# Two small remainders in one tile of a routed expert layer, with the second expert's weights fetched

## The chip, the cores and the metric

The kernel runs on one core of a Trainium2 chip. The metric is the device time of one execution in microseconds; the time before is the median of three runs.

## What is computed

The input `x` (4 x 256 tokens, 256 channels) first gets a gated mixing term, and then a gated expert layer. The second one is what matters here. There are T = 1024 tokens, H = 256 channels, E = 32 experts with M = 176 inner channels, and each token goes to 6 experts:

```python
scores = jax.nn.sigmoid(xf @ w_router)
# 4 of 8 groups of experts by scores + corr_bias, then 6 experts among these
combine = zeros((T, E)).at[arange(T)[:, None], topk_idx].add(topk_w)
g = einsum('th,ehm->etm', xf, gate_w)
u = einsum('th,ehm->etm', xf, up_w)
eo = einsum('etm,emh->eth', silu(g) * u, down_w)
routed = einsum('te,eth->th', combine, eo)
shared = silu(xf @ sh_gate_w) * (xf @ sh_up_w) @ sh_down_w
x = x + tanh(g_ffn[0]) * (routed + shared)
```

Everything is in float32. How many tokens an expert gets is known only when the kernel runs.

## The kernel before

The first part (about a third of the time) computes the mixing term, the router, the choice of experts and the shared expert. The expert with the most tokens in the first half is treated apart: all 1024 tokens go through it (`gate_up_busy`, `turn_h_busy`, `down_busy`). All other pairs of token and expert are written as rows to a buffer in HBM, `rows_dram`, each expert's rows in a region of its own (L429 `place`, indirect DMAs of GpSimd). On VectorE a table is worked out (L1074 to L1116): tile t of 128 rows belongs to expert `tiles[0, t]` and begins at row `tiles[1, t]`. An expert's remainder under 128 rows takes a tile of its own. The tiles are cut into rounds of `ROUND = 8`, and `last`, the number of the last round, comes from the table at run time: `last_i` is the number of entries of `round_at` (16, 24, ...) that lie under the number of tiles, and `load_last` (L255) adds 1.

The main loop goes tile by tile. All weights lie in SBUF (`wgu`, `wd`), and the engines work one behind the other:

- SyncE (SP queue), and ScalarE's queue up to tile 31, loads the 128 rows of tile t into one of 8 buffers (L259 `load`), once tile t - 8 has been transposed (`s_xT`) and taken (`s_taken`). From round `HELD = 4` on this is the loop at L354, all on SP.
- TensorE, at step t (L806 `iteration`), does four things in this order: `transpose_x` of tile t + 2 (L736), `gate_up` of tile t + 1 (L742, two matmuls of 352 columns, `pG`), `turn_h` of tile t (L750) and `down` of tile t - 1 (L756, two matmuls of 256 columns, `pY`). Rounds 0 and 1 are written out, then comes a loop over all rounds that are possible with an `If` in it (L837), then the last round.
- ScalarE copies the transposed rows (L547), applies silu (L552) and scales the result with the token's weight (L559 `scale_y`).
- VectorE, at step t (L1174 `turn`), copies the transposed h of tile t (L1134), gates tile t + 1 (L1130), and takes from tile t + 1's rows the weights and the token numbers (L1136 `take`, the lines L1140 and L1143, which count `s_taken` up).
- GpSimd adds each tile's result to the rows of one of three sums in HBM, by token number (L436 `add`, L445, an indirect DMA with addition). Two adds into one sum may not overlap, so each waits until the one before it into its sum has landed.

After the last round SP reads the three sums back (L367), VectorE adds them (L1197, L1203), and the output is written (L371).

Another piece that the steps use: at L313 `weights_of_busy` fetches one expert's weights by a number read at run time, in four DMAs on SP.

The reference's own inputs, counted apart from the kernel, give this: without the expert treated apart there are 32 full tiles, 8 remainders of more than 64 tokens and 16 remainders of 1 to 64 tokens, so 56 tiles in 7 rounds.

## Time and profile before

| | us |
|---|---|
| median of three runs | 258.53 (258.03 to 259.87) |
| profiled execution, its own time | 258.77 |
| its span | 256.9 |
| TensorE busy | 219.3 (85%) |
| GpSimd busy | 157.4 (61%) |
| VectorE busy | 129.4 (50%) |
| ScalarE busy | 80.0 (31%) |

The span is what the profiler saw between the first and the last instruction; the execution's own time is 1.9 us longer. Busy times are sums over an engine's instructions. PE is TensorE, PEld its weight loads, DVE VectorE, ACT ScalarE, POOL GpSimd, SP SyncE. Matmuls are recorded with modelled ends that overlap; in the chain of work the overlap is taken out. A float32 matmul stands as two records.

### The profile page before, as it was taken

How to read it: one execution, taken by the hardware profiler on the slowest of the kernel's cores; microseconds unless marked ns; L12 is line 12 of the kernel's file. 1: busy time of each engine (PE TensorE's matmuls, PEld its weight loads, DVE VectorE, ACT ScalarE, POOL GpSimd, SP SyncE). 2: the span in 40 equal slices, each digit the busy share in tenths (PEclk: the TensorE clock that was granted, in tenths of full speed). 3: DMA queues.
4: the chain of work that ended last, by engine and by line, in shares of the span. 5: the costliest groups of instructions: out<-in, count | busy, mean ns of one | idle time of the engine just before them, and what ended most of it. 6: DMA issues, size and time to landing. Idle time of an engine off the chain costs nothing.

```text
span 256.9 us, 5093 instructions
## 1 busy us (share of the span) xinstructions
PE 219.3 (85%) x1043; PEld 170.9 (67%) x1044; DVE 129.4 (50%) x528; ACT 80.0 (31%) x222; POOL 157.4 (61%) x188
## 2 busy tenths in 40 slices
PE   7996987994799789999999999999999998996000
PEld 6895776882677467877777777778777776774000
DVE  2898886929554444434443444434343443343334
ACT  3636121011010124343434344344444433442000
POOL 6352888787878873528468488566575665475300
PEclk9779799997599999999999999999999999999555
DMA  6999999999997649999998768777667675257767
GB/s 200 250 260 278 407 376 331 332 373 292 318 351 255 195 151 337 253 303 214 249 231 158 126 112 154 121 121 119 107 117 108 110 119 81 35 64 153 175 168 260
DMA packets 41018, 53.72 MB, mean 209 GB/s; under 512 B 5134, under 2 KB 35438, under 8 KB 40998
## 3 DMA queue, kind: packets, MB, share of 16 engines
q1 hardware_dynamic: 25520, 30.99, 41.7%
q0 software_dynamic: 11280, 18.36, 35.7%
q10 hardware_dynamic: 4198, 4.15, 5.9%
q8 instruction: 7, 0.11, 0.3%
q14 instruction: 13, 0.11, 0.1%
HBM read 31.72 MB, written 21.77 MB: 208 GB/s over the span
## 4 chain that ended last, share of the span: by engine, by line
PE 61%; DVE 17%; DMA 8%; issue 5%; another core or an unknown queue 4%; POOL 4%; ACT 1%; SPq 0%; ACTq 0%; POOLq 0%; DVEq 0%
PE pG L742 26%; PE pY L756 18%; PE pX L736 5%; DMA sum_dram<-xnT,idx 5%; PE pH L750 5%; PE pG L765 3%; PE pY L692 2%; PE pY L784 2%; DMA wgu<-sum_dram 2%; POOL rows_dram L432 1%; DMA wij<-in_L_xattn_W_dram 1%; PE pH L773 1%; DVE wgu L1013 1%; POOL rstd L418 1%
## 5 line engine op out<-in xcount | busy, mean ns | idle before, releaser
L445 POOL DMA_INDIRECT sum_dram<-xnT,idx x56 | 86.7, 1548 | 57.2 <-ACT xnT L559 30.8
L742 PE MATMUL pG<-wgu,sdown 128*128 x224 | 75.8, 461 | 1.4 <-issue 1.4
L432 POOL DMA_INDIRECT rows_dram<-rows,row_i x48 | 47.5, 989 | 18.3 <-issue 11.3
L756 PE MATMUL pY<-wd,sup 88*128 x224 | 57.5, 379 | 0.0
L1134 DVE COPY sup<-pH 88x256 f32<-88x256 f32 x56 | 23.5, 420 | 59.0 <-PE pH L750 51.3
L742 PEld LDWEIGHTS pG<-wgu,sdown 128*128 128x128 f32 x224 | 38.5, 191 | 13.9 <-issue 2.0
L559 ACT ACTIVATE xnT<-pY,wt 128x256 f32<-128x256 f32 x56 | 26.5, 473 | 54.1 <-issue 22.4
L756 PEld LDWEIGHTS pY<-wd,sup 88*128 88x128 f32 x224 | 38.0, 190 | 3.2 <-issue 0.2
L750 PEld LDWEIGHTS pH<-ident,sgate 128*88 128x88 f32 x112 | 18.0, 161 | 13.6 <-DVE sgate L1130 0.5
L552 ACT ACTIVATE sgate<-pG 128x176 f32<-128x176 f32 x56 | 17.8, 317 | 27.1 <-PE pG L742 26.0
L547 ACT ACTIVATE sdown<-pX 128x256 f32<-128x256 f32 x56 | 21.0, 377 | 4.9 <-PE pX L736 4.5
L750 PE MATMUL pH<-ident,sgate 128*88 128x128 f32 x112 | 21.5, 273 | 0.0
L1130 DVE TENSOR_TENSOR sgate<-sgate,pG 128x176 f32<-128x176 f32 x56 | 18.1, 323 | 0.1
L692 PE MATMUL pY<-sdown,wgu 128*128 128x256 f32 (+1 forms) x48 | 13.9, 448 | 4.9 <-DVE wgu L1013 3.4
L681 PE MATMUL pG<-xnT,sgate 128*128 128x256 f32 (+1 forms) x48 | 13.8, 413 | 3.6 <-DVE wgu L1013 3.6
L692 PEld LDWEIGHTS pY<-sdown,wgu 128*128 128x128 f32 (+1 forms) x48 | 10.6, 225 | 7.9 <-DVE wgu L1013 4.2
L519 ACT ACTIVATE wgu<-pG 128x256 f32<-128x256 f32 (+1 forms) x12 | 4.6, 383 | 29.8 <-PE pG L681 18.4
L681 PE MATMUL pG<-xnT,sup 128*128 128x256 f32 (+1 forms) x48 | 13.8, 415 | 0.0
L681 PEld LDWEIGHTS pG<-xnT,sgate 128*128 128x128 f32 (+1 forms) x48 | 8.5, 192 | 5.7 <-DVE wgu L1013 4.5
L736 PEld LDWEIGHTS pX<-ident,rows 128*128 128x128 f32 x56 | 10.6, 196 | 2.0 <-issue 0.7
L736 PEld LDWEIGHTS pX<-ident,xg 128*128 128x128 f32 x56 | 10.9, 195 | 1.3
L736 PE MATMUL pX<-ident,rows 128*128 128x128 f32 x56 | 10.9, 278 | 0.3 <-issue 0.3
(183 smaller groups left out, 246.2 us busy)
## 6 DMA issues: line engine op xcount, KB each, us to landing
wgu<-in_L_ffn_gate_w_dram SPq DMA_DIRECT2D x8, 704.0 KB, 10.0
wgu<-in_L_ffn_up_w_dram SPq DMA_DIRECT2D x8, 704.0 KB, 13.0
wd<-in_L_ffn_down_w_dram SPq DMA_DIRECT2D x8, 640.0 KB
sum_dram<-zeros POOLq DMA_DIRECT2D x3, 1152.0 KB
wgu<-sum_dram SPq DMA_DIRECT2D x12, 256.0 KB, 3.9
xg<-rows_dram SPq DMA_DIRECT2D x16, 144.5 KB
rows<-rows_dram ACTq DMA_DIRECT2D x16, 144.5 KB
rows_dram<-zeros SPq DMA_DIRECT2D x8, 289.0 KB, 4.5
```

The lines of the kernel that those rows point to most:

```text
L432: pool.indirect_dma_start(rows_dram[:, :], bass.IndirectOffsetOnAxis(ap=row_i[:, j, k:k + 1], axis=0), lines[:, j * ROW:j * ROW + LINE], N ...
L445: pool.indirect_dma_start(sums_dram[into[s]][:, :], bass.IndirectOffsetOnAxis(ap=idx[:, s:s + 1], axis=0), y[s], None, compute_op=ALU.add) ...
L547: nc.scalar.activation(xT[:, par, :, :].rearrange("p k t -> p (k t)"), pX[par][:, 0:K * P], ACT.Copy).then_inc(s_xTc, 1)
L559: nc.scalar.activation(y[s], pY[s % 2][:, 0:H], ACT.Copy, scale=wt[:, s:s + 1]).then_inc(s_yc, 1)
L681: ins = nc.tensor.matmul(pG[u % 2][0:m, i * GROUP * P:(i + 1) * GROUP * P], w[:, k, c], xnT[:, k, b * GROUP * P:(b + 1) * GROUP * P], star ...
L692: ins = nc.tensor.matmul(pY[j % 2][:, 0:H], sh[0:m, b % 2, i, (j % GROUP) * P:(j % GROUP + 1) * P], sdown[0:m, i, :], start=(i == 0), stop ...
L736: ins = nc.tensor.transpose(pX[par][:, k * P:(k + 1) * P], xg[s][:, 0:H].rearrange("t (p k) -> t k p", k=K)[:, k, :], ident[:, :])
L742: ins = nc.tensor.matmul(pG[par][:, 0:2 * M].rearrange("t (g m) -> t g m", g=2), xT[:, par, k, :], wgu[:, bass.ds(e, 1), :, k, :].rearrang ...
L750: ins = nc.tensor.transpose(pH[par][0:MI, i * P:(i + 1) * P], h[:, par, :].rearrange("t (p i) -> t i p", i=I)[:, i, :], ident[:, :])
L756: ins = nc.tensor.matmul(pY[par][:, 0:H], hT[0:MI, par, i, :], wd[:, bass.ds(e, 1), i, :], start=(i == 0), stop=(i == I - 1))
L1130: V.tensor_tensor(h[:, par, :], sg[:, par, :], pG[par][:, M:2 * M], ALU.mult).then_inc(s_h, 1)
L1134: V.tensor_copy(hT[0:MI, par, :, :].rearrange("p i t -> p (i t)"), pH[par][0:MI, 0:I * P]).then_inc(s_hTc, 1)
```

## The change

Remainders of up to `SIDE = 64` tokens no longer take a tile of 128 rows each. The last round but one (`last - 1`) is a round of 8 shared tiles: the upper 64 rows belong to one expert, the lower 64 rows to another one, whose table entries are at `SHARED + s` and `SHARED + 8 + s`. Full tiles and remainders over 64 tokens take the other rounds (small ones beyond 16 too). The number of rounds is then that of the whole tiles, divided by 8 and rounded up, and one more: with the counts above 40 / 8 + 1 = 6.

In a shared tile, `gate_up_sides` and `down_sides` do each matmul of a whole tile as two matmuls of 64 columns of the weight side, one for each expert, the second into output partitions 64 to 127 with `tile_position=(0, 64)`. The first expert's weights are read from where all lie; those of the second are fetched again from HBM into fixed places of SBUF: three places for gate and up (`own_gu`, 2 DMAs of 176 KB each time), two for down (`own_d`, 2 DMAs of 160 and 16 KB). These places overlay tables of the routing that are no longer needed (`choice` in place of eleven tensors). The first three pairs of gate and up and the first two of down are issued before round 4; the rest stand in SP's program between the row loads of the final round (`load_final`).

A shared tile's rows come in two DMAs, its weights and indices are taken in four VectorE instructions in place of two, its result is scaled by two ScalarE instructions of 64 partitions and added by two indirect DMAs of 64 rows, in the order of sums `INTO_SIDES`. The table needs a fourth segment and some more steps. TensorE's last three rounds, and the last two of the other engines, are written out behind the loop.

The core of the diff ("..." where lines are left out):

```diff
-    LEAST = -(-(PAIRS - T) // (P * ROUND)) - 1
+    SIDE = P // 2
+    SHARED = P - 2 * ROUND
+    LEAST = HELD + 1
...
-    SEGS = 3
+    SEGS = 4
...
+    INTO_SIDES = [(q + 2) % SUMS for q in range(2 * ROUND)]
-    INTO_LAST = [2, 0, 1, 2, 0, 1, 0, 1]
+    INTO_LAST = [0, 2, 1, 2, 0, 1, 0, 1]
...
+        own_gu = [lines[:, JH * ROW:JH * ROW + 2 * K * M].rearrange("p (g k m) -> p g k m", g=2, k=K),
+                  *(choice[:, at:at + 2 * K * M].rearrange("p (g k m) -> p g k m", g=2, k=K) for at in (0, 2 * K * M))]
+        own_d = [choice[0:MI, at:at + I * H].rearrange("p (i c) -> p i c", i=I)
+                 for at in (4 * K * M, 4 * K * M + I * H)]
...
-            return eng.value_load(last_i[0:1, 0:1], min_val=LEAST - 1, max_val=ROUNDS - 2) + 1
+            return eng.value_load(last_i[0:1, 0:1], min_val=LEAST - 2, max_val=ROUNDS - 2) + 2
...
+            def load_sides(t, s):
+
+                sp.wait_ge(s_xT, t - (XRING - 1))
+                sp.sem_inc(s_passed, 1)
+                sp.wait_ge(s_taken, t - (XRING - 1))
+                sp.sem_inc(s_passed, 1)
+                for side in range(2):
+                    entry = SHARED + side * ROUND + s
+                    v = sp.value_load(tiles[1:2, entry:entry + 1], min_val=0, max_val=4 * (E // 2 * PAIR - SIDE) + 2)
+                    at = v >> 2
+                    sp.dma_start(xg[s][side * SIDE:(side + 1) * SIDE, :],
+                                 rows_dram[bass.ds(at, SIDE), 0:ROW]).then_inc(s_load[s], 16)
+
+            def load_final(s):
+
+                v = sp.value_load(tiles[1:2, bass.ds((last - 1) * ROUND + s, 1)], min_val=0, max_val=4 * (E // 2 * PAIR - P) + 2)
+                at = v >> 2
+                sp.wait_ge(s_xT, last * ROUND + s - (XRING - 1))
+                sp.sem_inc(s_passed, 1)
+                sp.wait_ge(s_taken, last * ROUND + s - (XRING - 1))
+                sp.sem_inc(s_passed, 1)
+                sp.dma_start(xg[s], rows_dram[bass.ds(at, P), 0:ROW]).then_inc(s_load[s], 16)
+
+            def own_expert(s):
+                entry = SHARED + ROUND + s
+                return sp.value_load(tiles[0:1, entry:entry + 1], min_val=0, max_val=E - 1)
+
+            def own_gate_up(s):
+
+                e = own_expert(s)
+                if s >= 3:
+                    sp.wait_ge(s_gu, (last - 1) * ROUND + s - 2)
+                    sp.sem_inc(s_passed, 1)
+                for g, w in enumerate((gate_w, up_w)):
+                    sp.dma_start(own_gu[s % 3][:, g, :, :].rearrange("p k m -> p (k m)"),
+                                 w[bass.ds(e, 1)].rearrange("e (p k) m -> p (e k m)", k=K)).then_inc(s_owngu[s % 3], 16)
+
+            def own_down(s):
+
+                e = own_expert(s)
+                if s >= 2:
+                    sp.wait_ge(s_y, (last - 1) * ROUND + s - 1)
+                    sp.sem_inc(s_passed, 1)
+                for ps in EVEN:
+                    sp.dma_start(own_d[s % 2][ps, :, :].rearrange("p i c -> p (i c)"),
+                                 down_w[bass.ds(e, 1)].rearrange("e (p i) c -> p (e i c)", i=I)[ps, :]).then_inc(s_ownd[s % 2], 16)
+
             last = load_last(sp)
+            for s in range(3):
+                own_gate_up(s)
+            for s in range(2):
+                own_down(s)
             with sp.Fori(HELD, ROUNDS) as i:
-                with sp.If(i < last + 1):
+                with sp.If(i < last - 1):
                     for s in range(ROUND):
                         load(sp, i * ROUND + s, s, all_placed=True)
+            for s in range(ROUND):
+                load_sides((last - 1) * ROUND + s, s)
+            for n in range(-2, ROUND - 1):
+                if n + 2 < ROUND:
+                    load_final(n + 2)
+                if 3 <= n + 4 < ROUND:
+                    own_gate_up(n + 4)
+                if 2 <= n + 1:
+                    own_down(n + 1)
 
...
+            def add_side(t, q):
+
+                prior = [n for n in range(-ROUND, q) if (INTO[n] if n < 0 else INTO_SIDES[n]) == INTO_SIDES[q]][-1]
+                pool.wait_ge(s_add[prior % YRING], 16 * (last - 1) + (16 * (prior // YRING + 1) if prior >= 0 else 0))
+                pool.wait_ge(s_yc, t + 1)
+                pool.sem_inc(s_go, 1)
+                pool.indirect_dma_start(sums_dram[INTO_SIDES[q]][:, :], bass.IndirectOffsetOnAxis(ap=idx_own[:, q:q + 1], axis=0),
+                                        y[q % YRING][0:SIDE, :], None, compute_op=ALU.add).then_inc(s_add[q % YRING], 16)
...
-            with pool.Fori(1, ROUNDS - 1) as i:
-                with pool.If(i < last):
+            with pool.Fori(1, ROUNDS) as i:
+                with pool.If(i < last - 1):
                     for s in range(ROUND):
                         add(i * ROUND + s, s, i)
+            for q in range(2 * ROUND):
+                add_side((last - 1) * ROUND + q // 2, q)
             for s in range(ROUND):
-                add(last * ROUND + s, s, last, INTO_LAST)
+                add_final(last * ROUND + s, s)
...
+            def scale_y_sides(t, s):
+                act.wait_ge(s_y, t + 1)
+                act.wait_ge(s_taken, t + 1)
+                for side in range(2):
+                    q, ps = 2 * s + side, slice(side * SIDE, (side + 1) * SIDE)
+                    act.wait_ge(s_add[q % YRING], (last - 1) * 16 + 16 * (q // YRING))
+                    ins = nc.scalar.activation(y[q % YRING][0:SIDE, :], pY[s % 2][ps, 0:H], ACT.Copy, scale=wt[ps, s:s + 1])
+                ins.then_inc(s_yc, 1)
...
+            def gate_up_sides(t, s, e):
+
+                par = s % 2
+                pe.wait_ge(s_xTc, t + 1)
+                pe.wait_ge(s_owngu[s % 3], 32 * (s // 3 + 1))
+                for k in range(K):
+                    nc.tensor.matmul(pG[par][0:SIDE, 0:2 * M].rearrange("t (g m) -> t g m", g=2), xT[:, par, k, 0:SIDE],
+                                     wgu[:, bass.ds(e, 1), :, k, :].rearrange("p e g m -> p (e g) m"),
+                                     start=(k == 0), stop=(k == K - 1))
+                    ins = nc.tensor.matmul(pG[par][SIDE:P, 0:2 * M].rearrange("t (g m) -> t g m", g=2), xT[:, par, k, SIDE:P],
+                                           own_gu[s % 3][:, :, k, :], start=(k == 0), stop=(k == K - 1),
+                                           tile_position=(0, SIDE))
+                ins.then_inc(s_gu, 1)
...
+            def down_sides(s, e):
+
+                par = s % 2
+                pe.wait_ge(s_ownd[par], 32 * (s // 2 + 1))
+                for i in range(I):
+                    nc.tensor.matmul(pY[par][0:SIDE, 0:H], hT[0:MI, par, i, 0:SIDE], wd[:, bass.ds(e, 1), i, :],
+                                     start=(i == 0), stop=(i == I - 1))
+                    ins = nc.tensor.matmul(pY[par][SIDE:P, 0:H], hT[0:MI, par, i, SIDE:P], own_d[par][:, i, :],
+                                           start=(i == 0), stop=(i == I - 1), tile_position=(0, SIDE))
+                ins.then_inc(s_y, 1)
...
             with pe.Fori(2, ROUNDS - 1) as i:
-                with pe.If(i < last):
+                with pe.If(i < last - 2):
                     iteration(i)
-            e_last = iteration(last, tiles=ROUND)
+            _, e_side = iteration(last - 2, shared=1)
+            e_side, e_final = iteration(last - 1, shared=2, e_next=e_side)
+            e_last, _ = iteration(last, shared=3, e=e_side, e_next=e_final)
...
-            link(V.tensor_scalar(cnt_i[:, 2, :], counted[:, 1, :], float(P - 1), None, ALU.add))
+            V.tensor_scalar(cnt_i[:, 2, :], counted[:, 1, :], float(P - 1 - SIDE), None, ALU.add)
+            link(V.tensor_scalar(cnt_i[:, 3, :], counted[:, 1, :], float(P - 1), None, ALU.add))
...
+            V.scalar_tensor_tensor(whole[:, :], tend[:, 3, E - 1:E], -2.0 * ROUND, tend[:, 2, E - 1:E],
+                                   op0=ALU.add, op1=ALU.max)
+            V.tensor_scalar(small_at[:, 0:1], part_f[:, :], tend[:, 2, E - 1:E], side_of[:, 3:4], ALU.is_ge, ALU.mult)
+            link(V.tensor_scalar(small_at[:, 1:2], tend[:, 2, E - 1:E], -float(P), side_of[:, 0:1], ALU.add, ALU.mult))
+            link(V.tensor_tensor(small_at[:, 2:3], small_at[:, 0:1], small_at[:, 1:2], ALU.add))
...
+            V.tensor_scalar(shift[:, 0:1], found[:, 3:4], side_of[:, 1:2], 0.0, ALU.mult, ALU.max)
+            V.tensor_scalar(shift[:, 1:2], found[:, 3:4], 0.0, side_of[:, 2:3], ALU.max, ALU.mult)
+            V.tensor_scalar(shift[:, 2:3], found[:, 3:4], 0.0, 4.0 * HOME, ALU.is_equal, ALU.mult)
...
+            def take_sides(t, s, i):
+
+                es = [dve.value_load(tiles[0:1, entry:entry + 1], min_val=0, max_val=E - 1)
+                      for entry in (SHARED + s, SHARED + ROUND + s)]
+                dve.wait_ge(s_load[s], 16 * i + 32)
+                for side, e in enumerate(es):
+                    ps = slice(side * SIDE, (side + 1) * SIDE)
+                    V.tensor_copy(wt[ps, s:s + 1], xg[s][ps, bass.ds(e + H, 1)])
+                for side in range(2):
+                    entry, ps = SHARED + side * ROUND + s, slice(side * SIDE, (side + 1) * SIDE)
+                    ins = V.tensor_scalar(idx_own[:, 2 * s + side:2 * s + side + 1], xg[s][ps, H + E:ROW].bitcast(I32),
+                                          high[ps, entry:entry + 1], low[ps, entry:entry + 1], ALU.min, ALU.max)
+                ins.then_inc(s_taken, 1)
```

## Rows read from the trace of the kernel before

**Rows 1.** Busy time of the engines by stage: us, five engines, clock, DMA share, GB/s.

```profile
core 0: us, PE busy (x) PEld busy (x) DVE busy (x) ACT busy (x) POOL busy (x), PEclk, DMA share, GB/s
180.00:200.00 20.00, 20.00 (x98) 15.58 (x97) 8.64 (x33) 8.67 (x25) 12.38 (x9) 1.00 0.69 112
```

**Rows 2.** Chain that ended last, 179 to 187 us: start, us, what.

```profile
181.21 0.87 PE pY L756 x4
182.08 0.22 PE pX L736 x2
182.30 1.19 PE pG L742 x4
183.49 0.22 PE pH L750 x2
183.71 0.86 PE pY L756 x4
```

**Rows 3.** VectorE's part of one tile, timeline: start, us, line and operation, idle before.

```profile
181.59 0.32 DVE L1130 TENSOR_TENSOR sgate<-sgate,pG 128x176 f32<-128x176 f32 x1
182.22 0.15 DVE L1140 COPY wt<-rows 128x1 f32 x1 [0.31 <-issue]
182.36 0.27 DVE L1143 TENSOR_SCALAR idx<-rows,high,low 128x1 int32<-128x1 int32 x1
```

**Rows 4.** SP's instructions for row loads, L274 and L261, 178 to 184 us: ns min/median/max.

```profile
L274 SPq DMA_DIRECT2D rows<-rows_dram x3: 332/332/333, 178.0 to 182.9; - x3
L261 SPq SEQ_ASSERT  x3: 18/18/18, 179.0 to 183.9; - x3
```

**Rows 5.** SP's queue at the one fetch of an expert's weights, timeline.

```profile
41.13 1.25 SPq L318 DMA_DIRECT2D wd<-in_L_ffn_down_w_dram  x2
42.41 0.07 SPq L321 DMA_DIRECT2D wgu<-in_L_ffn_gate_w_dram  x1
42.58 0.56 SPq L321 DMA_DIRECT2D wgu<-in_L_ffn_up_w_dram  x1
```

**Rows 6.** From the issue of a 256 KB DMA to its landing, L371 and then L367.

```profile
DMA to landing us min/median/max: 2.2/2.4/3.0
...
DMA to landing us min/median/max: 2.7/3.9/6.1
```

**Rows 7.** GpSimd's adds, timeline: start, us, idle before and what ended it.

```profile
118.82 1.55 POOL L445 DMA_INDIRECT sum_dram<-xnT,idx  x1 [0.30 <-issue]
120.67 1.55 POOL L445 DMA_INDIRECT sum_dram<-xnT,idx  x1 [0.30 <-issue]
234.40 1.55 POOL L445 DMA_INDIRECT sum_dram<-xnT,idx  x1 [0.72 <-ACT xnT L559]
241.27 1.55 POOL L445 DMA_INDIRECT sum_dram<-xnT,idx  x1 [2.79 <-DMA sum_dram<-xnT,idx]
```

**Rows 8.** TensorE's clock around two idle times, by stage (columns as in rows 1).

```profile
62.00:64.00 2.00, 0.46 (x2) 0.00 (x0) 1.90 (x13) 0.38 (x1) 1.15 (x3) 0.50 1.06 334
70.00:72.00 2.00, 2.00 (x7) 1.52 (x6) 0.48 (x1) 0.00 (x0) 1.72 (x3) 0.68 1.03 286
72.00:74.00 2.00, 2.00 (x10) 1.31 (x10) 0.34 (x1) 0.52 (x2) 1.67 (x4) 1.00 1.08 329
```

**Rows 9.** TensorE's wait in the table's stretch, timeline: start, us, idle before.

```profile
65.90 5.49 PE L692 MATMUL pY<-sdown,wgu 128*128 128x256 f32 x12 [3.43 <-DVE wgu L1013]
```

**Rows 10.** VectorE ahead of that wait, timeline.

```profile
62.77 0.16 DVE L1088 SCALAR_TENSOR_TENSOR need<-need 128x1 f32<-128x1 f32 x1
62.85 0.27 DVE L1089 TENSOR_SCALAR cur<-tbase,part_f 128x96 f32<-128x96 f32 x1
63.15 0.26 DVE L1090 TENSOR_TENSOR cur<-cur,past 128x96 f32<-128x96 f32 x1
```

**Rows 11.** Chain where TensorE leaves the loop over rounds: start, us, what.

```profile
213.66 0.87 PE pY L756 x4
...
215.83 1.45 PE pG L742 x4
```

More of the change, by code:

```diff
@@ L434, in place, with add @@
                 chain(pool.memset(wj_wide[:, :], 0.0))
-            def add(t, s, i, into=INTO):
-                prior = [n for n in range(-ROUND, s) if (INTO[n] if n < 0 else into[n]) == into[s]][-1]
+            def add(t, s, i):
+                prior = [n for n in range(-ROUND, s) if INTO[n] == INTO[s]][-1]
                 if isinstance(t, int) and prior < 0:
@@ L574, in _, with turn @@
             silu(0, 0)
-            def turn(i, s, left=ROUND, old=2, fetch=()):
+            def turn(i, s, left=ROUND, old=2, fetch=(), shared=0):
                 t = i * ROUND + s
@@ L583, in turn @@
                     load(act, n, n % ROUND)
-                if s:
+                if s and shared == 1 or not s and shared == 2:
+                    scale_y_sides(t - 1, (s - 1) % ROUND)
+                elif s and shared == 2:
+                    scale_y(t - 1, s - 1, True, last + 1)
+                elif s:
                     scale_y(t - 1, s - 1, old > 0, i)
@@ L592, in _ @@
             last = load_last(act)
-            with act.Fori(HELD, ROUNDS - 1) as i:
-                with act.If(i < last):
+            with act.Fori(HELD, ROUNDS) as i:
+                with act.If(i < last - 1):
                     for s in range(ROUND):
@@ L597, in _ @@
             for s in range(ROUND):
-                turn(last, s, ROUND - s)
-            scale_y(last * ROUND + (ROUND - 1), ROUND - 1, True, last)
+                turn(last - 1, s, left=2 * ROUND, shared=1)
+            for s in range(ROUND):
+                turn(last, s, ROUND - s, shared=2)
+            scale_y(last * ROUND + (ROUND - 1), ROUND - 1, True, last + 1)
         @block.tensor
@@ L804, in _, with iteration @@
             gate_up(0, 0, e_first)
-            def iteration(i, first=False, tiles=None):
-                e = e_next = None
+            def iteration(i, first=False, shared=0, e=None, e_next=None):
                 for s in range(ROUND):
-                    left = tiles - s if tiles else ROUND
+                    left = ROUND - s if shared == 3 else ROUND
+                    sides = shared == 2 and s < ROUND - 1 or shared == 1 and s == ROUND - 1
+                    final = shared == 3 or shared == 2 and s == ROUND - 1
                     t = i * ROUND + s
@@ L829, in iteration @@
                             pe.wait_ge(s_byc, J - 2 + t)
-                        down(t - 1, (s + 1) % 2, e_old)
-                return e
+                        if shared == 2 and s > 0 or shared == 3 and s == 0:
+                            down_sides((s - 1) % ROUND, e_old)
+                        else:
+                            down(t - 1, (s + 1) % 2, e_old)
+                return e, e_next
             iteration(0, first=True)
@@ L1172, in _, with turn @@
             gate(0, 0)
-            def turn(i, s, left=ROUND, first=False):
+            def turn(i, s, left=ROUND, first=False, shared=0):
                 t = i * ROUND + s
@@ L1184, in _ @@
             with dve.Fori(1, ROUNDS - 1) as i:
-                with dve.If(i < last):
+                with dve.If(i < last - 2):
                     for s in range(ROUND):
@@ L1188, in _ @@
             for s in range(ROUND):
-                turn(last, s, ROUND - s)
+                turn(last - 2, s, shared=1)
+            for s in range(ROUND):
+                turn(last - 1, s, shared=2)
+            for s in range(ROUND):
+                turn(last, s, ROUND - s, shared=3)
             for b in range(B):
```

131 lines of the change are left out of this document (86 added, 45 removed).

## The prediction

> **What bounds the kernel now.** I read the engines' busy time by stage first. In the tile loop TensorE is busy all 20.00 of 20 us at full clock while VectorE and ScalarE stand at under half and GpSimd at 12.4 [rows 1]. The chain that ended last says the same: a tile is `down` 0.87, the transposes of x 0.22, `gate_up` 1.19 and the transposes of h 0.22, with no gap between them, and the next `down` starts 183.71 - 181.21 = 2.50 us after this one [rows 2]. So in this stage a tile is worth 2.50 us, whatever the other engines do. Behind the loop there is a tail of adds and sums, which the change leaves as it is: the last round's adds keep their order from its third tile on.
>
> **What is removed.** With the reference's counts, 7 rounds become 6: 8 x 2.50 = 20.0 us less.
>
> **What a shared tile costs on TensorE.** It has each matmul of `gate_up` and `down` twice, with all 352 or 256 columns streamed each time. One after the other, the halves add 1.19 + 0.87 = 2.06, and a shared tile takes p = 4.56 us. Fully side by side they add nothing, p = 2.50. No row shows a matmul on half the array's columns. The nearest rows are whole ones, of two records each [rows 2]. I take p = 3.0, for this reason: if halves of different experts can overlap but instructions start in program order, only the second record of one half overlaps with the first of the next, so eight records take five steps in place of four, 0.25 x 2.06 = 0.5 more. Eight tiles: +4.0, with the ends 0 and +16.5.
>
> Rows 2 show only whole-width matmuls, one at a time. The Trainium skill (TensorEngine Tiling (Array Packing), Key Properties) says that tiles on different parts of the array load weights and multiply in parallel, and that a change of the tiling mode drains the engine, which a shared tile would do four times. By the first, the sum below would have p = 2.50 and end at 261.1; the second has no price there. No run so far shows either.
>
> **When the second expert's weights come.** This is the step that decides. Places 0 to 2 for gate and up, and 0 and 1 for down, are filled long before. All later ones stand in SP's program behind a row load, and that load waits until VectorE has taken the rows of a tile. Let r be the moment when TensorE comes to `down` of tile k - 1. In the trace r is 181.21 and the take of tile k + 1 ends at 182.36 + 0.27 = 182.63 [rows 2, 3]. A shared tile's take has one more read of a number (0.31), one more copy (0.15) and one more index instruction (0.27), partly overlapped: it ends at r + 2.1. SP issues the row load 0.27 later (182.9) for 0.33, and then needs 0.66 until it has read the next number (178.0 + 0.33 to 179.0) [rows 4]. Four weight DMAs with a number read at run time took 43.14 - 41.13 = 2.0, so 0.5 each [rows 5]. Gate and up of tile k + 3: issued by r + 2.1 + 0.27 + 0.33 + 0.66 + 1.0 = r + 4.4, the last one begun at r + 4.0. A DMA of 256 KB landed 2.4 to 3.9 after its issue (medians of two lines) [rows 6]; I take 3.0 for two of 176 KB, so r + 7.0. Down of tile k stands behind them: 0.66 + 1.0 more, the last piece (16 KB) begun at r + 5.6, landing 2.3 later, r + 7.9. Where there is no gate and up ahead of it, r + 6.2.
>
> TensorE wants this down p after r. So from the third shared tile on it comes 7.9 - 3.0 = 4.9 late. Now p by p, from r = 0 at `down` of tile 31: gate and up of shared tile 3 land at 7.0, wanted at 4.1: 2.9 late. Down 2: asked for from r = 8.7, lands at 16.6, wanted at 11.7: 4.9. Down 3: SP is still in the set before until 14.7, needs 4.3 for its own, last piece begun at 18.6, lands 20.9, wanted 19.6: 1.3. Down 4: from r = 19.6, lands 27.5, wanted 23.9: 3.6. Down 5: none. Down 6: from 30.5, lands 36.7, wanted 33.2: 3.5. Sum +16.2 us. With the same reckoning p = 2.50 gives 18.0 and p = 4.56 gives 10.9. The bounds of the fetch at p = 3.0: 11.9 with 0.33 per weight DMA, 0.5 per number and landings of 2.2 and 2.4; 23.9 with 0.6 and landings of 3.9 [rows 4 to 6]. The stalled waits hold nothing else up: VectorE and ScalarE have done tile k + 1 by then, and the bytes (8 x 528 KB) are small beside the DMA share of 0.69 at 112 GB/s, when the round is twice as long [rows 1].
>
> **TensorE's clock.** Around an idle time of 3.43 us the clock was 0.50, that is 1.2 GHz in place of 2.4, and its mean of 0.68 over 70 to 72 us puts the rise at 71.3 [rows 8, 9]: from 65.90 on, half of 5.4 us lost, 2.7. The round has four or five waits of 1.3 to 4.9 us. I take one such loss, +2.7; ends 0 and three, 8.1.
>
> **The table.** The new steps stand ahead of the instruction for which TensorE waits 3.43 us already (L1013, the gate of the shared expert) [rows 9], so they are on the path. An instruction with a chained one behind it costs 0.3, an unchained one 0.08 to 0.1 [rows 10]: three chained (0.8, with `small_at`), five unchained (0.4), and ten that are 128 columns wide in place of 96 (0.2), less one removed (0.1): +1.3. The steps behind the wait (0.4) are hidden by the `down` of the shared expert.
>
> **Leaving the loop.** The `down` before the exit and the next `gate_up` lie 2.17 apart in place of 1.09 [rows 2, 11]. That is there before and after; six rounds are now skipped in place of three, +0.5 as an estimate from half of this 1.1; ends 0 and 1.1.
>
> **The adds.** 16 half adds take the place of 16. Back to back one takes 1.85 (120.67 - 118.82), and one that waited for the add before it into its sum came 6.87 behind it, over three sums 2.3 each [rows 7]. 16 x 2.3 = 37 us at most, against a round of 20 + 4 + 16 = 40: hidden. In a round without late weights they would be the limit, at 16 x 1.85 = 30.
>
> **The sum**, against the profiled execution's 258.77: - 20.0 + 4.0 + 16.2 + 2.7 + 1.3 + 0.5 = 263.5. That execution was 0.24 over the median: **263.2**.
>
> **Rivals.** *The halves run one after the other*: 258.77 - 20.0 + 16.5 + 10.9 + 1.8 + 1.3 (half a clock loss, since the waits are shorter) = 269.3, 269 by the median. For it: no row shows overlap on the array. *Side by side and a quick fetch (the other side)*: p = 2.50, and SP issues weight DMAs as fast as row DMAs (0.33) that land after 2.2 to 2.4, no clock loss: late by 13.7, 258.77 - 20.0 + 13.7 + 1.8 = 254.3, 254 by the median. For it: bytes are few, and the busy expert's gate DMA shows 0.07 [rows 5]. It decides from where all waits for weights together fall under 20.0 - 1.8 - 4.0 = 14.2 at p = 3.0. If no weight came late at all, 240 to 256; rows 4 to 6 leave no room for that. *The round isn't saved*, because the kernel counts otherwise than the reference: 7 rounds with one of them shared, 258.5 + 4 + 16 + 4.5 = 283.
>
> **How the numbers follow.** A measurement of this kernel tells about 1% (2.6 us) from no change. The forecast, late weights with halves that overlap partly or fully, has 0.42 (its own range 260 to 268). One after the other 0.24. Quick fetch and overlap 0.20. Between it and the forecast, within 1%, 0.13. Round not saved 0.01. Faster by over 1% comes from the quick fetch and the little for which nothing is late: 0.21. Within 1%: 0.14. Slower: 0.65. The range goes from the quick fetch to one after the other with its waits a little longer, 254 to 271.
>
> **What would show it.** In the profile after: 48 tiles, the last `gate_up` of whole tiles 8 fewer; waits of TensorE at `gate_up_sides` of shared tile 3 and at `down_sides` of tiles 2, 4 and 6 ended by DMAs of weights, 3 to 5 us each; starts of the half matmuls 0.15 apart in pairs if they overlap, 0.3 if not; clock 0.5 in a part of the round; L1013's wait at 65.9 about 1.3 longer. Wrong if those waits sum to under 14 us, or if the row load ahead of the weights turns out not to hold them.

## The result and the profile after

The changed kernel takes 280.28 us (median), beside 259.2 for the kernel before on the same chip: ratio 1.078, 95% interval 1.067 to 1.090. It is slower by some 20 us, and the time lies beyond the upper end of the forecast range. One of its four executions took 533.43 us, for which there is no trace; ratios and intervals, here and below, leave out executions that fell into a slower state of the chip, and medians count all of them.

| | before | after |
|---|---|---|
| profiled execution, us | 258.77 | 281.48 |
| its span, us | 256.9 | 279.5 |
| mean granted clock | 0.924 | 0.891 |
| 128-token tiles of the loop stage | 56 | 40 whole, 8 shared |

The page's busy tenths show it at once. Each digit is a fortieth of the span, 7.0 us; from the 27th on TensorE has gaps, and its granted clock falls with them. Before, those slices were 20.00 busy of 20 at full clock [rows 1].

```profile
PE   7996988962899999999899699983838285998000
PEclk9999799999599999999999979997868686899555
```

The timeline of TensorE, filtered to the starts that follow an idle time (start, us, line and operation, idle before and what ended it):

```profile
160.40 0.50 PE L848 MATMUL pX<-ident,rows 128*128 128x128 f32 x2 [2.52 <-issue]
187.00 0.51 PE L865 MATMUL pG<-wgu,sdown 128*64 x1 [0.84 <-ACT sdown L644]
194.89 0.84 PE L865 MATMUL pG<-wgu,sdown 128*64 x1 [4.66 <-DMA rows<-in_L_ffn_up_w_dram]
207.38 0.68 PE L891 MATMUL pY<-wd,sup 88*64 x1 [5.96 <-DMA choice<-in_L_ffn_down_w_dram]
221.89 0.68 PE L891 MATMUL pY<-wd,sup 88*64 x1 [5.99 <-DMA choice<-in_L_ffn_down_w_dram]
234.04 0.68 PE L891 MATMUL pY<-wd,sup 88*64 x1 [4.37 <-DMA choice<-in_L_ffn_down_w_dram]
```

Four waits, 21.0 us together, at `gate_up_sides` of shared tile 3 and at `down_sides` of tiles 2, 4 and 6: the places of the forecast. Each ends with a DMA of the second expert's weights. Busy time by stage (columns as in rows 1) shows what the waits do to the clock:

```profile
180.00:190.00 10.00, 9.16 (x56) 5.30 (x54) 4.24 (x17) 3.16 (x10) 5.28 (x4) 1.00 0.57 96
190.00:200.00 10.00, 5.34 (x26) 2.19 (x27) 2.01 (x10) 2.25 (x6) 2.86 (x2) 0.66 0.64 130
200.00:210.00 10.00, 4.04 (x22) 1.69 (x20) 2.09 (x8) 1.56 (x5) 2.85 (x2) 0.76 0.54 129
210.00:220.00 10.00, 5.90 (x30) 2.45 (x30) 3.19 (x12) 2.69 (x7) 5.70 (x4) 0.84 0.50 99
220.00:230.00 10.00, 7.78 (x36) 3.75 (x36) 1.89 (x7) 3.29 (x8) 3.24 (x3) 0.72 0.32 67
230.00:240.00 10.00, 5.96 (x22) 3.15 (x24) 1.44 (x6) 1.64 (x4) 4.37 (x4) 0.66 0.35 68
```

The matmul that ends a wait takes 0.68 or 0.84 where the same one took 0.42 to 0.51 at full clock. The DMA share falls to a third from 220 us on while the waits go on, so bytes are not what is short; the second experiment tests that.

The 22.6 us between the spans can be placed by the starts of the same tile's `gate_up` in both traces:

| `gate_up` | start after, us | later than before by |
|---|---|---|
| first of the loop | 95.70 | 2.9 |
| ahead of the exit from the loop | 155.61 | 3.3 |
| behind the exit | 161.40 | 6.6 |
| first shared tile | 180.45 | 8.1 |
| last of the 48 tiles | 252.95 | 43.2 (209.76 before) |

Before then goes on for the eight tiles that the change saves, 20.9 us. The shared stretch takes 43.2 - 8.1 = 35.1 more than whole tiles did: 21.0 of waits for weights, 0.8 of one for ScalarE, 8 x 0.67 = 5.4 of the shared tiles themselves (below), and 7.9 are left. They fit the half clock: in the profile some 17 us of TensorE's work behind the four waits ran at a granted clock of 0.50 (after the first of them from 194.89 to 198.4), which costs up to half of that, 8.6.

### The profile page after: what moved, and what is told of

Read it like the earlier page. It is cut to its first block, busy times and chain, and to the rows that moved or that the text cites. A ratio compares the mean times of both kernels' runs of the same rounds, so it can differ in the third digit from the quotient of the medians.

```text
span 279.5 us, 4976 instructions
## 1 busy us (share of the span) xinstructions
PE 215.5 (77%) x1011; PEld 156.2 (56%) x1012; DVE 127.0 (45%) x529; ACT 76.1 (27%) x206; POOL 155.9 (56%) x188
## 4 chain that ended last, share of the span: by engine, by line
PE 48%; DVE 13%; DMA 13%; SPq 10%; issue 9%; POOL 2%; another core or an unknown queue 2%; DVEq 1%; ACTq 1%; ACT 0%; POOLq 0%
PE pG L854 13%; PE pY L882 7%; DMA sum_dram<-xnT,idx 6%; PE pG L905 3%; PE pX L848 3%; PE pG L793 3%; SPq L379 3%; DMA choice<-in_L_ffn_down_w_dram 3%; PE pH L876 3%; PE pY L804 3%; PE pG L865 2%; PE pY L891 2%; SPq L377 2%; PE pY L924 2%
## 5 line engine op out<-in xcount | busy, mean ns | idle before, releaser
L521 POOL DMA_INDIRECT sum_dram<-xnT,idx x32 | 49.6, 1551 | 38.3 <-DMA sum_dram<-xnT,idx 17.4
L854 PE MATMUL pG<-wgu,sdown 128*128 x160 | 56.9, 480 | 1.5 <-issue 1.0
L882 PE MATMUL pY<-wd,sup 88*128 x160 | 41.2, 380 | 0.0
L530 POOL DMA_INDIRECT sum_dram<-xnT,idx_own x16 | 22.8, 1426 | 32.8 <-ACT xnT L664 26.4
L854 PEld LDWEIGHTS pG<-wgu,sdown 128*128 128x128 f32 x160 | 28.5, 198 | 11.5 <-issue 3.4
L656 ACT ACTIVATE xnT<-pY,wt 128x256 f32<-128x256 f32 x40 | 19.0, 474 | 40.2 <-PE pX L848 14.5
L882 PEld LDWEIGHTS pY<-wd,sup 88*128 88x128 f32 x160 | 27.2, 190 | 2.5 <-issue 0.3
L891 PE MATMUL pY<-wd,sup 88*64 x32 | 11.4, 492 | 16.3 <-DMA choice<-in_L_ffn_down_w_dram 16.3
L865 PE MATMUL pG<-wgu,sdown 128*64 x32 | 14.0, 570 | 5.5 <-DMA rows<-in_L_ffn_up_w_dram 4.7
L540 POOL DMA_INDIRECT sum_dram<-xnT,idx x8 | 12.5, 1561 | 8.2 <-issue 5.3
L664 ACT ACTIVATE xnT<-pY,wt 64x256 f32<-64x256 f32 x16 | 7.5, 471 | 28.4 <-PE pY L893 28.3
```

Source lines behind the costliest of these rows:

```text
L521: pool.indirect_dma_start(sums_dram[INTO[s]][:, :], bass.IndirectOffsetOnAxis(ap=idx[:, s:s + 1], axis=0), y[s], None, compute_op=ALU.add) ...
L530: pool.indirect_dma_start(sums_dram[INTO_SIDES[q]][:, :], bass.IndirectOffsetOnAxis(ap=idx_own[:, q:q + 1], axis=0), y[q % YRING][0:SIDE, ...
L656: nc.scalar.activation(y[s], pY[s % 2][:, 0:H], ACT.Copy, scale=wt[:, s:s + 1]).then_inc(s_yc, 1)
L854: ins = nc.tensor.matmul(pG[par][:, 0:2 * M].rearrange("t (g m) -> t g m", g=2), xT[:, par, k, :], wgu[:, bass.ds(e, 1), :, k, :].rearrang ...
L865: nc.tensor.matmul(pG[par][0:SIDE, 0:2 * M].rearrange("t (g m) -> t g m", g=2), xT[:, par, k, 0:SIDE], wgu[:, bass.ds(e, 1), :, k, :].rear ...
L882: ins = nc.tensor.matmul(pY[par][:, 0:H], hT[0:MI, par, i, :], wd[:, bass.ds(e, 1), i, :], start=(i == 0), stop=(i == I - 1))
```

## The experiments

Waits are named by the matmuls that wait: G3 is `gate_up_sides` of shared tile 3, D2 `down_sides` of shared tile 2.

### No late weights

```diff
-                if 3 <= n + 4 < ROUND:
-                    own_gate_up(n + 4)
-                if 2 <= n + 1:
-                    own_down(n + 1)
...
-                pe.wait_ge(s_owngu[s % 3], 32 * (s // 3 + 1))
+                pe.wait_ge(s_owngu[s % 3], 32)
```

(and the same for `s_ownd`.)

> Edit to the changed kernel: the second expert's weights are fetched only for shared tiles 0 to 2 (gate, up) and 0 and 1 (down); the later shared tiles read what then lies in these places, so their result is left wrong; all else stays. Theory A (TensorE waits for late weights, and its clock falls in these waits): the four waits of 4.66, 5.96, 5.99 and 4.37 us go, and most of the clock loss of about 8 us with them: 280 - 21 - 8 = 251 us (248 to 255), clock 1.0 through the shared round. Rival B (the shared round is slow for another reason: half-width matmuls, 16 adds, changed tiling mode): the waits move to something else and the time stays over 262.

Measured: 259.41 beside 263.64, ratio 0.976 (0.970 to 0.983). Against after's 1.078, the late weights cost 0.102 of 259.2, 26 us, more than the eight tiles saved. Of these 26, 21 are the waits, and some 5 are left for the clock, which stands at 1.00 from 180 to 230 us in this trace. The trace also answers what a shared tile costs. The chain of one shared tile, from the transposes of x of one tile to those of the next (start, us, what; the rows of 0.01 between them are the second halves):

```profile
195.07 0.44 PE pX L844 x2
195.50 0.44 PE pG L861
...
195.95 0.29 PE pG L861
...
196.84 0.39 PE pH L872 x2
197.23 0.36 PE pY L887
...
197.59 0.21 PE pY L887
...
198.24 0.43 PE pX L844 x2
```

3.17 us per tile (198.24 - 195.07), with no idle. A half matmul adds 0.01 to its partner: they are fully side by side. What is added to the 2.50 of a whole tile, 0.67, sits where whole and half widths meet: transposes of x 0.44 in place of 0.22, first half of `gate_up` 0.44 in place of the 0.29 of the next, transposes of h 0.39 in place of 0.22, first half of `down` 0.36 in place of 0.21.

### All fetches, not awaited

```diff
-                pe.wait_ge(s_owngu[s % 3], 32 * (s // 3 + 1))
...
-                                           own_gu[s % 3][:, :, k, :], start=(k == 0), stop=(k == K - 1),
+                                           wgu[:, 0, :, k, :], start=(k == 0), stop=(k == K - 1),
```

(and the same for `down`; SP waits for each fetch before it overwrites the place.)

> Edit to the changed kernel: all weight fetches are made as before by SP, in the same places of its queue, but TensorE reads expert 0's resident weights for the second half and never waits for a fetch (the second expert's result is so left wrong). Theory A: the bytes and SP's work harm nothing, only the waiting does: the time is that of the run without late fetches, within 1.5 us. Rival C (the 4 MB more take DMA time from row loads and adds): at least 5 us over that run.

Measured: 259.3 beside 263.64, ratio 0.985 (0.979 to 0.991). Issuing all fetches and moving their bytes costs 0.009 (2.3 us) more than leaving out the late ones, with intervals that overlap; the rest of the 0.102, ten times as much, is the waiting.

### The fetches ahead of the row loads

```diff
-            for n in range(-2, ROUND - 1):
-                if n + 2 < ROUND:
-                    load_final(n + 2)
-                if 3 <= n + 4 < ROUND:
-                    own_gate_up(n + 4)
-                if 2 <= n + 1:
-                    own_down(n + 1)
+            for n in range(2, ROUND):
+                if n + 1 < ROUND:
+                    own_gate_up(n + 1)
+                own_down(n)
+                load_final(n - 2)
+            for n in range(ROUND - 2, ROUND):
+                load_final(n)
```

> Edit to the changed kernel: in SP's program the late fetches stand ahead of the final round's row loads, so that each waits only until its own place is free. Theory A: down of tile k is asked for after down k - 2 and no longer after the take of tile k + 1, but a set of row load, gate, up and down still takes SP 4.3 to 5 us against 2.8 of a shared tile: about half of the 21 us of waits goes, with some of the clock loss, 266 to 270 us. Rival C (a fetch is slow by itself): 277 us or more.

Measured: 266.62 beside 263.64, ratio 1.010 (1.004 to 1.015). The same instructions in another order take away 0.068, some 18 us, though the late weights are not gone. In the timeline three waits are left, 7.6 us in place of 21.0, all for up weights:

```profile
192.07 0.51 PE L865 MATMUL pG<-wgu,sdown 128*64 x1 [0.43 <-DMA rows<-in_L_ffn_up_w_dram]
198.50 0.84 PE L865 MATMUL pG<-wgu,sdown 128*64 x1 [3.19 <-DMA choice<-in_L_ffn_up_w_dram]
211.13 0.84 PE L865 MATMUL pG<-wgu,sdown 128*64 x1 [3.96 <-DMA rows<-in_L_ffn_up_w_dram]
```

So what stood ahead of the weights in SP's queue did hold them, as the forecast had it.

### The second expert's weights copied inside the chip

The weights of all experts lie in `wgu` and `wd` already. Here no fetch goes out; VectorE copies gate and up, ScalarE down.

```diff
-                if 3 <= n + 4 < ROUND:
-                    own_gate_up(n + 4)
-                if 2 <= n + 1:
-                    own_down(n + 1)
...
+                V.tensor_copy(own_gu[k % 3].rearrange("p g k m -> p (g k m)"),
+                              wgu[:, bass.ds(e, 1), :, :, :].rearrange("p e g k m -> p (e g k m)")).then_inc(s_owngu[0], 1)
...
+                nc.scalar.activation(own_d[k % 2].rearrange("p i c -> p (i c)"),
+                                     wd[:, bass.ds(e, 1), :, :].rearrange("p e i c -> p (e i c)"), ACT.Copy).then_inc(s_ownd[0], 1)
```

> Edit to the changed kernel: no fetch at all; the second expert's weights are copied inside SBUF from where all experts' weights lie, gate and up by VectorE (704 columns), down by ScalarE (512 columns), two to three tiles ahead. The whole computation is done. Theory A: the waits go; VectorE has about 3 us of work in a shared tile, so the round takes 8 x 3 us: 252 us (249 to 256), faster than the kernel before. Rival B: over 262.

Measured: 257.06 beside 263.64, ratio 0.975 (0.969 to 0.981), as fast as the kernel without the late fetches. The copies take 0.53 to 0.56 us on VectorE and 0.63 on ScalarE, where those have slack. This is the whole computation, with nothing left out, and 2.5% faster than before (1.9 to 3.1%). One wait of after's timeline is still there: TensorE stands 2.52 us at the loop's exit and starts again at 159.92.

### Both kernels once more, on one chip

No edit; for traces side by side.

> The kernel before, unchanged, for a trace on the chip of the runs beside it. Expected: its own time within 1%, TensorE's first gate_up of the tile loop within 1 us of the trace before if that start is the same on any chip; if the 2.9 us by which the changed kernel's came later were mostly the chip, it comes 1.5 us or more later here too.

> The changed kernel, unchanged, on the same chip as the runs beside it. Expected: 1.07 to 1.09 of the kernel before; waits of TensorE for weights at shared tiles 3 (gate, up) and 2, 4, 6 (down), 21 us together, the same four as in the first trace. If it was chance which tiles waited (contention), the pattern is another one here.

Measured: 260.25 for before (two runs, 257.59 and 262.9), beside 258.5 for its other runs; 279.99 for after, ratio 1.081 (1.071 to 1.090). The four waits come back as 4.49, 5.78, 5.84 and 4.21. The table's instruction that TensorE waits for (VectorE's timeline, before and then after):

```profile
65.92 0.40 DVE L1013 TENSOR_TENSOR wgu<-wgu,pG 96x256 f32<-96x256 f32 x1
```

```profile
68.10 0.41 DVE L1168 TENSOR_TENSOR wgu<-wgu,pG 96x256 f32<-96x256 f32 x1
```

It starts 2.18 later. Taken from where this stretch begins (59.87 and 60.61 us), 6.05 has become 7.49: 1.4 by the table. The first `gate_up` of the loop starts at 91.84 and 95.41.

### Order of the halves

Built on the copying kernel: all matmuls of the first expert, then all of the second.

```diff
                                      start=(k == 0), stop=(k == K - 1))
+                for k in range(K):
...
                                      start=(i == 0), stop=(i == I - 1))
+                for i in range(I):
```

> Edit to the kernel with weights copied inside SBUF: in each shared tile both matmuls of the first expert stand ahead of both of the second one, in place of by turns. Theory D (two halves run side by side only where neighbouring matmuls lie on different halves of the array): little overlap is left, up to 2.06 us more in each of 8 shared tiles, 257 + 10 to 16 = 267 to 273 us on the chip of that run. Rival E (the engine pairs halves whatever their order in the program, within its queue): within 2 us of 257.

Measured: 257.16 beside 258.5, ratio 0.988 (0.983 to 0.994). The timeline of TensorE shows the pairs all the same:

```profile
199.01 0.51 PE L868 MATMUL pG<-wgu,sdown 128*64 x1
199.02 0.51 PE L872 MATMUL pG<-choice,sdown 128*64 128x352 f32 x1
199.35 0.46 PE L868 MATMUL pG<-wgu,sdown 128*64 x1
199.37 0.46 PE L872 MATMUL pG<-choice,sdown 128*64 128x352 f32 x1
```

The order in the program, and in its compiled form too, is A, A, A, A, B, B, B, B; the starts are A, B, A, B, 0.01 to 0.02 apart. The tile takes 3.18 (201.76 - 198.58, starts of L851). So halves meet whether or not they are neighbours, and the forecast's reason for p = 3.0 (a start in program order lets only some of the records overlap) falls. By program order, only the last of A and the first of B could overlap in this kernel, seven steps in place of four, and the tile would be longer by 3 x 0.29 + 3 x 0.21 = 1.5; it is longer by 0.01. The Trainium skill (TensorE: Matmul & The Clock Gate, The mechanism) has matmuls start strictly in program order; here the measurement says otherwise and decides. The ratio of this kernel is 0.013 above that of the copying kernel, on another chip; whether the order or the chip makes that is open.

### The loops cut to the rounds that run

The loops over rounds go to the largest count that any input can need and skip the body by an If. Here they end where these inputs end, first in the copying kernel, then in after, then in before.

```diff
-            with pe.Fori(2, ROUNDS - 1) as i:
+            with pe.Fori(2, HELD - 1) as i:
```

(and so on each engine.)

> Edit to the kernel with weights copied inside SBUF: every loop over rounds ends where these inputs' rounds end, so no round is skipped at its exit (other inputs could need more rounds; that possibility is left out). Theory F (each skipped round costs TensorE's sequencer some 0.4 us, so the exit 2.52 us idle, and the clock falls with it): 4 to 5 us less, 252 to 253 us, no half-clock gate_up behind the exit. Rival G (the idle time is the fetch of the code behind the loop): within 1 us of 257.

> Edit to the changed kernel alone: every loop over rounds ends where these inputs' rounds end, so none is skipped at its exit (the possibility of more rounds is left out). Theory F: the 2.52 us idle at the exit, the half-clock gate_up behind it and ScalarE's later exit (0.84) go, 5 to 7 us less than the changed kernel: 1.055 to 1.065 of the kernel before. The four waits for weights stay. Rival: the exit only moves time into the waits for weights, which are set by SP's loads: under 2 us less.

> Edit to the kernel before: the same, its loops end at round 5. Theory F: its exit skips three rounds and costs 1.08 us, its entry 0.45: 1 to 2 us less, 0.993 to 0.997. If loops as such cost more than their exits (fetch of code, registers), 4 us or more less here too, and then the shorter loops' gain says little of the change.

Measured: the copying kernel 245.02 beside 258.5, ratio 0.946 (0.934 to 0.958), where it had 0.975; after 271.63 beside 258.32, ratio 1.050 (1.040 to 1.060), where it had 1.078. Cutting the loops is worth 0.028 to 0.029 of 259, 7 to 8 us (by the intervals some 3 to 11), in both kernels of the change. The four executions of before with cut loops took 253.24 to 258.32, too far apart to tell a difference from its 258.32.

The traces tell more, if one counts from the first `gate_up` of the loop to the end of the span, and so leaves out the part ahead of it, whose length changes from one execution to the next:

| | first `gate_up`, us | from there to the end |
|---|---|---|
| before, twice | 92.80, 91.84 | 164.1, 163.9 |
| before, loops cut | 95.77 | 160.5 |
| copying | 96.17 | 157.0 |
| copying, loops cut | 93.45 | 148.3 |
| after, twice | 95.70, 95.41 | 183.8, 183.1 |
| after, loops cut | 94.68 | 174.6 |

So the loops cost before 3.5 us too, and both kernels of the change some 9. That is more than the 2.52 at TensorE's exit. The chain of after (start, us, what) shows what follows it:

```profile
157.01 0.87 PE pY L882 x4
157.88 2.52 issue
160.40 0.51 PE pX L848 x2
...
161.40 2.71 PE pG L854 x4
```

The first `gate_up` behind the exit takes 2.71 where the others take 1.19, 1.5 more, at a granted clock of 0.50 from 162 to 164 us. ScalarE's own exit keeps TensorE 0.84 at 187.00; with the loops cut this wait is gone. Whether a skipped round costs its branch or the fetch of code, no run here separates. With the loops cut the waits for weights are 17.6 in place of 21.0:

```profile
187.55 0.84 PE L865 MATMUL pG<-wgu,sdown 128*64 x1 [4.86 <-DMA rows<-in_L_ffn_up_w_dram]
199.18 0.42 PE L891 MATMUL pY<-wd,sup 88*64 x1 [2.75 <-DMA choice<-in_L_ffn_down_w_dram]
204.69 0.42 PE L891 MATMUL pY<-wd,sup 88*64 x1 [0.75 <-DMA choice<-in_L_ffn_down_w_dram]
```

Here D3 waits too, as the forecast had it (1.3 there). The 3.4 us less of waits are no clear gain: the two waits at G3 are alike (4.66 and 4.86), and D2 waits less mainly because TensorE, at half clock for longer, comes to it 8.9 us after G3 began and not 6.5.

### Matmuls that fill the waits

Built on after: 18 matmuls of 128 columns of `ident` into an unread part of PSUM ahead of each of the four waits, so that TensorE is busy while it waits.

```diff
+            def fill(par, n):
+                for _ in range(n):
+                    nc.tensor.matmul(pY[par][:, 3 * P:4 * P], ident[:, :], ident[:, :], start=True, stop=True)
...
+                if s in (2, 4, 6):
+                    fill(par, 18)
                 pe.wait_ge(s_ownd[par], 32 * (s // 2 + 1))
```

> Edit to the changed kernel: ahead of each of the four waits for weights (gate and up of shared tile 3, down of 2, 4 and 6) TensorE does 18 matmuls of 128 columns into unused PSUM columns, about 3.9 us at full clock, in place of standing idle. Theory H (the waits cost twice: once themselves and once by the half clock behind them): the clock stays at 2.4 GHz through the shared round, the waits end when they did, and 5 to 8 us less than the changed kernel, 1.05 to 1.06. Rival: the clock behind the waits costs nothing on the path, since the next fetch is waited for anyway: within 2 us of it.

Measured: 272.95 beside 258.32, ratio 1.057 (1.049 to 1.065), 0.024 below after's second measurement, 6.2 us; with both intervals some 3 to 9. More work on TensorE makes the kernel faster, since it keeps the clock. Its stages (columns as in rows 1):

```profile
190.00:200.00 10.00, 9.01 (x67) 6.31 (x66) 3.19 (x12) 1.96 (x5) 4.42 (x4) 1.00 0.61 135
200.00:210.00 10.00, 6.65 (x36) 3.13 (x38) 1.59 (x6) 2.96 (x7) 3.40 (x3) 0.88 0.51 118
210.00:220.00 10.00, 10.00 (x73) 6.91 (x70) 2.35 (x8) 2.37 (x6) 3.77 (x4) 0.95 0.37 85
```

1.00, 0.88 and 0.95 stand where after had 0.66, 0.76 and 0.84, and 1.00 follows up to 240 us. One part of the gain may be chance. Behind the loop's exit, which the edit doesn't touch, the clock stayed at 1.00 this time, and `gate_up` took 1.45 in place of 2.71:

```profile
158.56 1.45 PE L854 MATMUL pG<-wgu,sdown 128*128 x4 [0.49 <-ACT sdown L644]
```

That is 1.3 of the difference between the two profiled executions; how the other executions of either kernel stand at this place, no trace shows.

### A version that beats both

The copying kernel with the rounds that always run outside the loops' Ifs, and one If around each loop. Unlike the kernels with cut loops it leaves no rounds out that another input could need.

```diff
-            with pe.Fori(2, ROUNDS - 1) as i:
-                with pe.If(i < last - 2):
-                    iteration(i)
+            iteration(2)
+            with pe.If(last > HELD + 1):
+                with pe.Fori(HELD - 1, ROUNDS - 1) as i:
+                    with pe.If(i < last - 2):
+                        iteration(i)
```

> Edit to the kernel with weights copied inside SBUF, valid for all inputs that it was valid for: the rounds that always run stand outside the loops, and one If around each loop jumps over all of it where no further round is needed. Theory F: one jump in place of six skipped rounds, so as fast as with the loops cut short, 0.94 to 0.955 of the kernel before. If more code costs its fetch, 0.96 to 0.975, with TensorE idle at its start for 1 us or more.

Measured: 245.53 beside 258.32, ratio 0.950 (0.942 to 0.959). TensorE is busy from the first tile to the last but a few, the exit and the shared round included (columns as in rows 1):

```profile
92.00:160.00 68.00, 68.00 (x321) 52.59 (x321) 28.36 (x107) 27.60 (x80) 42.29 (x34) 0.98 0.92 211
160.00:190.00 30.00, 30.00 (x170) 18.76 (x168) 17.35 (x61) 15.76 (x41) 20.10 (x14) 1.00 0.64 109
190.00:215.00 25.00, 25.00 (x135) 16.52 (x134) 11.71 (x43) 14.05 (x36) 20.03 (x14) 1.00 0.44 61
```

Sharing tiles and leaving the loops with one jump gain 5% together. Sharing alone, with the loops as they were, gave 2.5%; with the loops cut in both kernels it is worth 12 us (160.5 and 148.3 in the table above). Of the 0.128 between after (1.078) and this kernel, 0.103 is how the second expert's weights come, and 0.025, a fifth, is how the loops are left.

## Why the prediction went wrong, step by step

The side was right (slower), the mechanism was right, and the sum was short by 18 us against the profiled execution (263.5 and 281.48). The steps that failed are sizes of terms: the wait for late weights (+16.2, measured 21.0), TensorE's clock, taken as one loss for four or five waits (+2.7, measured 6.2), and the exit from the loop (+0.5, measured 4.3). These three make 12.1 of the 18.

| term | forecast | measured |
|---|---|---|
| eight tiles fewer | -20.0 | -20.0, 2.50 each (before's exit is counted in the last line) |
| shared tile | +4.0 | +5.4 |
| late weights | +16.2 | +21.0 |
| clock | +2.7 | +6.2 (3 to 9) behind these waits |
| table | +1.3 | +1.4 |
| loop exit | +0.5 | +4.3 on TensorE |

These terms add up to 258.77 - 20.0 + 5.4 + 21.0 + 6.2 + 1.4 + 4.3 = 277.1, of the profiled 281.48. Of the other 4.4, 1.7 are the rest of the 7.9 of half clock and 1.5 lie ahead of the loop: its first `gate_up` starts 2.9 later, of which the table explains 1.4. In kernels that all have the new table it starts anywhere from 92.1 to 98.6 us, and with the old table from 91.8 to 95.8. What moves it is not settled, and neither is the last 1.2.

**Late weights: the places right, the size short by 4.8.** The forecast had 2.9, 4.9, 1.3, 3.6 and 3.5 us at G3, D2, D3, D4 and D6; measured were 4.66, 5.96, 0, 5.99 and 4.37. SP's timeline around the fetch for D2, where r, the start of `down` of shared tile 1, is 198.03:

```profile
200.78 0.34 SPq L390 DMA_DIRECT2D rows<-rows_dram  x1
202.01 0.34 SPq L403 DMA_DIRECT2D choice<-in_L_ffn_gate_w_dram  x1
202.44 0.38 SPq L403 DMA_DIRECT2D choice<-in_L_ffn_up_w_dram  x1
203.82 0.87 SPq L413 DMA_DIRECT2D choice<-in_L_ffn_down_w_dram  x2
205.97 0.36 SPq L390 DMA_DIRECT2D xg<-rows_dram  x1
```

The take ended at 200.51, r + 2.5 (forecast r + 2.1). The row load follows 0.27 later for 0.34: right. Where SP reads a number at run time between two DMAs, 0.9 (201.12 to 202.01) and 1.0 (202.82 to 203.82) pass from the end of one issue to the start of the next, in place of 0.66. The weight DMAs took 0.34 to 0.44, below the forecast's 0.5. The last piece, issued at 204.29, landed at 207.14, 2.9 later in place of 2.3, and TensorE began 0.24 after that. In all r + 9.4 in place of r + 7.9. The two that were too small, the read and the landing, had been taken from row loads and from a stretch with other sizes [rows 4, 6]. From one row load to the next SP needs 205.97 - 200.78 = 5.2 us, against 3.17 for a tile: the queue itself is slower than TensorE, so some tiles must wait, and which ones can differ: D3 waits in one trace and not in the other.

The forecast also put nothing for SP's own work on the shared tiles' rows: two numbers read and two DMAs for each tile, 2.8 us (168.64, 171.41 and 174.18 are starts of `load_sides` in after). From 166.0 to 187.3 us SP did nothing else, without a pause. With the loops cut it was this work that held G3's fetch, and not the take: the take that the load ahead of it waits for ended at 180.84, the load went out 2.3 later (VectorE's timeline, then SP in the chain):

```profile
180.29 0.55 DVE L1334 TENSOR_SCALAR idx_own<-rows,high,low 64x1 int32<-64x1 int32 x2
```

```profile
183.12 0.35 SPq L390
```

In after itself both came together (SP ready at 188.9, the take over at 189.37).

**The shared tile: the number near, the reason wrong.** p = 3.17, where 3.0 stood. It is not that half of the overlap is lost; all of it is there (starts 0.01 apart), and 0.67 goes to the four changes between whole and half width. The Trainium skill (TensorEngine Tiling (Array Packing), Key Properties) states both: tiles on different parts of the array run in parallel, and a change of mode drains the engine. The trace agrees: the pairs run together, and the extra time, 0.15 to 0.22 us, stands at the four changes of width and nowhere else; that it is the drain itself is not shown. The forecast had the first with p = 2.50 and left the drains at nothing; 2.50 and four changes of 0.17 are the measured 3.17. That the assumed 3.0 came near was luck. The rival of halves one after the other is out.

**The clock: counted once, came four times.** Each of the four waits is longer than the 3.43 us that had cost 2.7 before [rows 9], and each left half clock behind it, which cost 1.5 to 2 us each (6.2 by the filling matmuls, 7.9 by the trace, over four). The forecast had four or five waits in its own text and took one loss for them. Its upper end, 8.1, holds the measured 6.2.

**The loop exit: no row of this size.** Before, three skipped rounds cost 1.09 [rows 11]; half of that for three more was +0.5. The trace of after has 3.3 more between the `gate_up` on both sides of the exit (155.61 to 161.40, less 2.50), 1.5 of half clock in the second one (2.71 less 1.19) and 0.84 at ScalarE's exit; before's own exit, 1.3 by the same reading, goes off: 4.3. The 1.5 of half clock is not there each time: `gate_up` took 1.45 behind before's exit [rows 11], 2.71 behind after's in both of its traces, and 1.45 behind the same 2.52 us in the kernel with filling matmuls. With it, the price of skipped rounds is not in proportion to their number. Cutting the loops of after was worth 0.028, 7 to 8 us, of which 5.6 are the exit (3.3 + 1.5 + 0.8).

**What was hidden stayed hidden.** GpSimd's half adds take 1.43 us each, and no TensorE wait in the shared stretch ends with them. The tail from TensorE's last matmul to the span's end is 21.7 before and 21.9 after. The bytes of the fetches cost at most 0.009 (the second experiment).

## What to carry to other kernels

Count how often the issuing queue can serve a set (here 5.2 us for a row load, four weight DMAs and the numbers read for them) and set it against the period of the consumer (3.2): where the queue is slower, more places only put the wait off. Ask of each fetch when its place came free and what stands ahead of it in its queue; the same instructions in another order were worth some 18 us, and data that already lies in SBUF can be copied by an engine with slack for 0.5 to 0.6 us. In this kernel each TensorE wait of 4 to 6 us cost 1.5 to 2 us more by the half clock behind it, so count one such loss for each wait. Jump over rounds that aren't needed with one If rather than through them.

## What the runs showed of the hardware

- Two matmuls on 64 of the array's columns each, in float32, run fully side by side: starts 0.01 us apart, 0.29 per pair of 352 columns, as long as one of whole width; also when the program has them in the order A, A, A, A, B, B, B, B.
- A change between whole and half width costs 0.15 to 0.22 us on TensorE.
- On SP 0.9 to 1.0 us lie between the issues of two DMAs where a number is read at run time in between, and each DMA whose address depends on such a number takes 0.34 to 0.44 (the fetches of after).
- Six skipped rounds of a loop held TensorE for 2.52 us. The `gate_up` behind them ran at 1.2 GHz in both traces of after (2.71 us), and at 2.4 GHz in the kernel with filling matmuls (1.45).
